# Moving an activation load off the weight queue, and sharing the last weight casts between ScalarE and VectorE, in a fused RWKV and ternary feed-forward kernel

## The chip, the cores and the metric

The kernel runs on all 8 cores of one Trainium2 chip. Each core works on its own 1024 tokens (plus 128 tokens of run-in for the recurrence), and no data passes between cores. The time is the device time of the slowest core in microseconds. Names used below: TensorE (PE in the profile), VectorE (DVE), ScalarE (ACT), GpSimd (POOL), and SyncE (SP), which only issues transfers.

## The reference

```python
xn = _layernorm(x)                                    # x: 2 x 4096 x 2048
prev = concatenate([xn[:, 1:2, :], xn[:, :-1, :]], axis=1)
xx = prev - xn
xk, xv, xr, xg = (xn + xx * tm for tm in (tm_k, tm_v, tm_r, tm_g))
r = xr @ Wr.T
k = xk @ Wk.T
v = xv @ Wv.T
g = sigmoid(xg @ Wg.T)
wkv = _wkv_scan(k, v, w, time_first)                  # recurrence over tokens
o = (sigmoid(r) * wkv * g) @ Wo.T
s = layernorm(o) * ln_g + ln_b
w_t = clip(round(weight / mean(abs(weight))), -1, 1)  # ternary weight
x = x + s * silu(xn @ (w_t * scale).T + bias)
```

All weights are 2048 x 2048 in float32, and the kernel multiplies in bfloat16.

## The kernel before

The program is a series of blocks. The first blocks compute the layernorm statistics, the mean of |weight|, and the four mixed inputs, which VectorE writes out through GpSimd's queue to the scratch tensors `sxk`, `sxv`, `sxr`, `sxg` in DRAM. Then come the two large matmul blocks that the change touches.

**The first matmul block** is `mm_group` (called at line 714). It runs three products in a row: k (weight `wk`, input `mov_kv` loaded from `sxk`), v (weight `wv`, the same buffer `mov_kv` loaded from `sxv`), and the ternary product (weight `wf`, input `xn_sb`, which is in SBUF already). Each product is done in two halves of 1024 output channels, so there are six halves. A half needs 16 weight tiles of 128 x 1024 (512 KB each). A tile is loaded into one of two staging buffers, `g1mwstg` (tile number `jj`, buffer `jj % 2`), and cast to bfloat16 into `g1wbf` (one buffer per half, two in all). In the k and v halves, even tiles are cast by VectorE (line 273) and odd ones by ScalarE (line 275). VectorE makes the ternary tiles alone (lines 265 to 270). The casts of a half may start when TensorE has finished the half before the last one (the table `release`).

One half is cut into groups: one 128-channel block by one chunk of tokens. A k or v half has 8 channel blocks of three chunks (512, 512 and 128 tokens), so 24 groups. A group is 16 matmuls into one PSUM bank, there are 8 banks, and ScalarE empties each (line 337) in order. ScalarE's program is written in order of groups: at the group at which a half's buffer comes free it first does its 8 casts of the next half's weights, then goes on emptying banks. TensorE can therefore be at most 8 groups ahead while ScalarE is at its casts.

The 16 tiles of `mov_kv` (288 KB each) are loaded in two parts. The dictionary `mov_sync={0: 8, 1: 8}` gives the first 8 tiles of each product to SyncE, counted by the semaphore `sl2`. ScalarE issues the other 8 (line 319), counted by `sl`, when it reaches the product's first group. Where SyncE's 8 stand differs: for k they are the first thing in its queue (line 213), ahead of the weight tiles; for v they come after all 32 weight tiles of v (line 220):

```python
for p, s in enumerate(specs):
    if p >= 1 and GRP0[p - 1] > 0 and movsync.get(p - 1):
        e.wait_ge(sem["smm"], b["smm"] + GRP0[p - 1])
        for ci in range(movsync[p - 1]):
            inc(e.dma_start(...), "sl2", 16)
    for h in range(2):
        ...   # the 32 weight tiles of product p, each waiting for the cast of tile jj - 2
```

TensorE waits for both counts before a product's first matmul.

**The second matmul block** (block at line 732) runs r, g and o with the weights `wr`, `wg` and `wo`. Here a slab is 512 output channels, so a product has four slabs and the block has 12. A slab is 16 weight tiles of 128 x 512 (256 KB each), in the two staging buffers `rgo_mw`, and 8 groups of 512 tokens, as many as there are PSUM banks. All 192 tiles are cast by ScalarE (line 828). ScalarE's order here is: 16 casts of the slab after next's buffer, then the 8 evictions of the slab before (lines 947, 954, 957). SyncE issues the weight tiles in order, tile `jj` after the cast of tile `jj - 2`. VectorE works through the list `v_events`: the recurrence first (`chain`, `q`, `sr`), then 32 products of `wkv` with the gate (`gmul`, line 913). The o product waits for the last of them.

After it come a layernorm of o and the final sum.

Of the kernel before, what the change touches and what calls it, by code (L numbers as in the profile page):

```python
# [23 lines left out]
def build_nc(C, T_OWN, LANE):  # L24
# [15 lines left out]
           for k in ("wk", "wv", "wr", "wg", "wo", "wf")}  # L40
# [15 lines left out]
    e0 = es0.enter_context  # L56

    sem = {n: e0(nc.semaphore(n)) for n in
           ("sl", "sl2", "sw0", "sw1", "scv", "scs", "smm", "sev", "st0",
            "st1", "sv", "ss", "sden", "srd", "sg0", "sg1")}  # L60
    cnt = {n: 0 for n in sem}

    def snap():
# [41 lines left out]
    def mm_group(specs, shared, pre=None, tail_sync=None, tail_scalar=None):  # L105
# [46 lines left out]
            CV[hh], CS[hh] = cv, cs_  # L152

        movpre = pre.get("mov_sl", {}) if pre else {}
        movsync = pre.get("mov_sync", {}) if pre else {}
        slt = {}
        slt2 = {}
        run_sl = cnt["sl"]
        run_sl2 = cnt["sl2"]
        for p, s in enumerate(specs):  # L160
            if p in movpre:
                slt[p] = movpre[p]
            elif s["mov_load"] is not None:
                run_sl += 16 * (CH - movsync.get(p, 0))
                slt[p] = run_sl
                if movsync.get(p):
                    run_sl2 += 16 * movsync[p]
                    slt2[p] = run_sl2

        signum = {}  # L170
        k = 0
# [32 lines left out]
        for p, s in enumerate(specs):  # L204
            if s["mov_load"] is not None and p not in movpre:
                mov_at.setdefault(GRP0[p], []).append(p)

        @blk.sync
        def _(e):
            for p, n in movsync.items():  # L210
                if GRP0[p] == 0:
                    for ci in range(n):
                        inc(e.dma_start(specs[p]["mov"][:, ci, :],
                                        specs[p]["mov_load"][ci, :, :]),
                            "sl2", 16)
            for p, s in enumerate(specs):
                if p >= 1 and GRP0[p - 1] > 0 and movsync.get(p - 1):
                    e.wait_ge(sem["smm"], b["smm"] + GRP0[p - 1])
                    for ci in range(movsync[p - 1]):
                        inc(e.dma_start(specs[p - 1]["mov"][:, ci, :],  # L220
                                        specs[p - 1]["mov_load"][ci, :, :]),
                            "sl2", 16)
                for h in range(2):
                    hh = 2 * p + h
                    for ic in range(CH):
                        jj = hh * CH + ic
                        if jj < preL:
                            continue
                        if jj >= 2:
                            eng, sname, tgt = castrec[jj - 2]  # L230
                            e.wait_ge(sem[sname], tgt)
                        inc(e.dma_start(mwstg[jj % 2][:, :],
                                        s["wt"][ic * 128:(ic + 1) * 128,
                                                (h * HC):(h + 1) * HC]),
                            "sw%d" % (jj % 2), 16)
            lp = len(specs) - 1
            if GRP0[lp] > 0 and movsync.get(lp):
                e.wait_ge(sem["smm"], b["smm"] + GRP0[lp])
                for ci in range(movsync[lp]):
                    inc(e.dma_start(specs[lp]["mov"][:, ci, :],  # L240
                                    specs[lp]["mov_load"][ci, :, :]),
                        "sl2", 16)
            if tail_sync is not None:
                tail_sync(e)

# [144 lines left out]
        @blk.tensor  # L390
        def _(e):
            for p, s in enumerate(specs):
                if s["mov_load"] is not None:
                    e.wait_ge(sem["sl"], slt[p])
                    if p in slt2:
                        e.wait_ge(sem["sl2"], slt2[p])
                if s.get("wait_y"):
                    e.wait_ge(sem["sv"], b["sv"] + nsig)
                for h in range(2):
                    hh = 2 * p + h  # L400
                    e.wait_ge(sem["scv"], CV[hh])
                    if CS[hh] > b0scs:
                        e.wait_ge(sem["scs"], CS[hh])
                    for oc in range(OH):
                        for tj, (t0, t1) in enumerate(s["tcs"]):
                            g = GRP0[p] + h * ngh[p] + oc * ntc[p] + tj
                            bank = ps[g % NBK]
                            if g >= NBK:
                                e.wait_ge(sem["sev"], b["sev"] + g - NBK + 1)
                            for ic in range(CH):  # L410
                                mm = e.matmul(bank[:, :t1 - t0],  # L411
                                              wbf[hh % 2][:, ic,
                                                          oc * 128:(oc + 1) * 128],
                                              s["mov"][:, ic, t0:t1],
                                              start=(ic == 0),
                                              stop=(ic == CH - 1))
                            inc(mm, "smm")
# [282 lines left out]
    with contextlib.ExitStack() as es:  # L700
        ec = es.enter_context
        mov_kv = ec(nc.sbuf_tensor("mov_kv", [128, CH, T_ALL], BF16))
        sh = {"es": es,
              "wbf": [g1wbf0,
                      ec(nc.sbuf_tensor("g1wbf1", [128, CH, HC], BF16))],
              "mwstg": g1mwstg,
              "mwm2": [ec(nc.sbuf_tensor("g1mwm2%d" % i, [128, HC], F32))
                       for i in range(2)],
              "rowst": [ec(nc.sbuf_tensor("g1row%d" % i, [128, T_ALL], F16))
                        for i in range(2)],  # L710
              "sigst": None,
              "g2st": [ec(nc.sbuf_tensor("g1g2s%d" % i, [128, 512], BF16))
                       for i in range(2)],
              "ps": [ec(nc.psum_tensor("g1ps%d" % i, [128, 512], F32))
                     for i in range(8)]}
        mm_group([
            spec(w_d["wk"], TC_ALL, "exp_row", mov_kv, mov_load=sxk,
                 store_ap=sek),
            spec(w_d["wv"], TC_ALL, "copy_row", mov_kv, mov_load=sxv,
                 store_ap=svd),  # L720
            spec(w_d["wf"], TC_OWN, "silu_g2", xn_sb, quant=True,
                 bias_vec=vec_sb["bfv"], store_ap=sg2),
        ], sh, pre=dict(preL=CH, recs=g1_pre_recs,
                        mov_sync={0: CH // 2, 1: CH // 2}))
    es_pre.close()
    es1.close()

# [4 lines left out]
    with contextlib.ExitStack() as es:  # L732
# [44 lines left out]
        CVs, CSs = [0] * NSS, [0] * NSS  # L777
        for ss in range(NSS):
            for ic in range(CH):
                cs_ += 1  # L780
                castrec.append(("S", "scs", cs_))
            CVs[ss], CSs[ss] = cv, cs_

        QLAG = 2
# [1 line left out]
        for i in range(CH + QLAG):  # L786
# [3 lines left out]
            if 0 <= cj < CH:  # L790
                v_events.append(("q", cj))
                v_events.append(("sr", cj))
        for k in range(NGp):
            v_events.append(("gmul", k))

        svord = {}
        i = 0
        for kind, l in v_events:
            if kind != "chain":
                i += 1  # L800
                svord[(kind, l)] = i
        NSV = i
# [60 lines left out]
        def _(e):  # L863
# [3 lines left out]
            for kind, l in v_events:  # L867
# [25 lines left out]
                elif kind == "q":  # L893
                    m = l % NROW
                    e.wait_ge(sem["srd"], b["srd"] + l + 1)
                    e.drain()
                    inc(e.tensor_tensor(wkv_sb[:, l, :],  # L897
                                        vvr[m][:, LANE:],
                                        ekr[m][:, LANE:],
                                        OP.mult), "sv")  # L900
                elif kind == "sr":
                    e.wait_ge(sem["sev"], b["sev"] + (l + 1) * ntc)
                    e.drain()
                    inc(e.tensor_tensor(wkv_sb[:, l, :],
                                        wkv_sb[:, l, :],
                                        sr_sb[:, l, :], OP.mult), "sv")
                else:
                    _p, sl_g, oc_g, tj_g = g_info(NR + l)
                    t0k, t1k = TC_OWN[tj_g]
                    ocg_k = sl_g * OSL + oc_g  # L910
                    e.wait_ge(sem["sev"], b["sev"] + NR + l + 1)
                    e.drain()
                    inc(e.tensor_tensor(wkv_sb[:, ocg_k, t0k:t1k],  # L913
                                        wkv_sb[:, ocg_k, t0k:t1k],
                                        sgst[l % NSG][:, :t1k - t0k],
                                        OP.mult), "sv")

        @blk.scalar
        def _(e):
# [298 lines left out]
```

## Time and profile before

| | us |
|---|---|
| median of the 2 timed runs shown | 1498.3 (1493.12 and 1503.47) |
| the profiled execution's own time | 1476.69 |
| its span, first to last instruction, slowest core (core 4) | 1475.2 |
| spans of the 8 cores | 1460.1 to 1475.2 |
| TensorE busy | 817.4 (55%) |
| VectorE busy | 524.6 (36%) |
| ScalarE busy | 494.7 (34%) |

No engine is busy for more than 55% of the span, so the table only says that engines wait for one another. Where they wait is read from the timeline. All rows are of core 4, the slowest. "SPq" and "ACTq" are the transfer instructions that SyncE and ScalarE issue; their time is that of the issuing, not of the transfer. A row's number in brackets is the idle time of the engine ahead of it and what ended it.

### The profile page before, as it was taken

To read this page: it belongs to the slowest core of one execution; us is meant where nothing else is said; L and a number is where in the kernel's file an instruction comes from. 1 tells how busy PE (TensorE), PEld (TensorE's weight loads), DVE (VectorE), ACT (ScalarE), POOL (GpSimd) and SP (SyncE) were. 2 spreads that over 40 slices of the span, in tenths; PEclk is the share of its full clock that TensorE was granted. 3 is DMA by queue.
4 is the path that set the end of the run, shared out by engine and by line. 5 is a ranking of instruction groups with operands and counts; after the bars stand their busy time and mean duration, and the time that the engine had idled before them with its cause. 6 is when DMAs were issued, how large, how long until landed. Compare 5 with 4: busy or idle time off the path is not lost. (4 is left out here: it accounts for less than half of the span.)

```text
span 1475.2 us, 11738 instructions; the slowest of 8 cores (1460.1 to 1475.2 us)
## 1 busy us (share of the span) xinstructions
PE 817.4 (55%) x3762; PEld 361.0 (24%) x3834; DVE 524.6 (36%) x499; ACT 494.7 (34%) x660; POOL 104.6 (7%) x196
## 2 busy tenths in 40 slices
PE   3532210064949049999990494561396879885200
PEld 1110000032524025554440231230142334331000
DVE  0158988200000000567304143875610000000597
ACT  5532222112122111112221355475453433328221
POOL 0002222000000000001111000000000000000011
PEclk9755555577979569999995697875698999999555
DMA  4448888664251741455216443434534444400387
GB/s 130 128 148 249 285 227 251 171 223 143 98 179 41 233 138 41 133 169 189 95 36 220 139 121 105 131 100 126 187 86 125 122 129 120 126 22 0 98 253 219
DMA packets 79070, 211.65 MB, mean 143 GB/s; under 512 B 11424, under 2 KB 11424, under 8 KB 79008
## 3 DMA queue, kind: packets, MB, share of 16 engines
q1 hardware_dynamic: 56736, 144.29, 34.0%
q0 software_dynamic: 15360, 53.49, 10.1%
q10 hardware_dynamic: 6912, 13.11, 2.6%
q8 instruction: 31, 0.51, 0.1%
q14 instruction: 31, 0.25, 0.1%
HBM read 166.81 MB, written 39.85 MB: 140 GB/s over the span
## 5 line engine op out<-in xcount | busy, mean ns | idle before, releaser
L981 PE MATMUL rgo_ps<-mov_rg,rgo_wbf 128*128 128x512 bf16 x1003 | 235.7, 396 | 184.2 <-ACT rgo_wbf L828 57.6
L411 PE MATMUL g1ps<-mov_kv,g1wbf 128*128 128x512 bf16 (+1 forms) x1505 | 255.1, 330 | 138.1 <-DMA mov_kv<-sxv 57.0
L828 ACT ACTIVATE rgo_wbf<-rgo_mw 128x512 bf16<-128x512 f32 x192 | 119.9, 633 | 266.5 <-DMA rgo_mw<-wr 92.0
L411 PEld LDWEIGHTS g1ps<-mov_kv,g1wbf 128*128 128x128 bf16 x1536 | 131.5, 100 | 261.7 <-issue 144.4
L981 PEld LDWEIGHTS rgo_ps<-mov_rg,rgo_wbf 128*128 128x128 bf16 x1024 | 103.4, 102 | 316.4 <-issue 206.1
L981 PE MATMUL rgo_ps<-wkv_sb,rgo_wbf 128*128 128x512 bf16 x502 | 116.2, 392 | 19.7 <-ACT sr_sb L957 11.2
L411 PE MATMUL g1ps<-xn_sb,g1wbf 128*128 128x512 bf16 x502 | 110.1, 379 | 0.5
L337 ACT ACTIVATE g1row<-g1ps 128x512 f16<-128x512 f32 (+1 forms) x96 | 45.3, 492 | 173.9 <-PE g1ps L411 165.2
L273 DVE CAST g1wbf<-g1mwstg 128x1024 bf16<-128x1024 f32 x24 | 16.7, 694 | 241.1 <-PE g1ps L411 91.9
L579 PE MATMUL ps_sc<-fs_a,ones 128*1 128x512 f16 x64 | 32.3, 608 | 83.1 <-ACT fs_a L624 83.1
L981 PEld LDWEIGHTS rgo_ps<-wkv_sb,rgo_wbf 128*128 128x128 bf16 x512 | 51.1, 100 | 84.7 <-issue 28.7
L411 PEld LDWEIGHTS g1ps<-xn_sb,g1wbf 128*128 128x128 bf16 x512 | 50.1, 98 | 60.2
L275 ACT ACTIVATE g1wbf<-g1mwstg 128x1024 bf16<-128x1024 f32 x24 | 25.3, 1056 | 108.6 <-DMA g1mwstg<-wv 72.0
L265 DVE TENSOR_SCALAR g1mwm<-g1mwstg,thr_sb 128x1024 f32<-128x1024 f32 x32 | 24.1, 754 | 104.2 <-PE g1ps L411 83.6
L624 ACT ACTIVATE fs_a<-g1mwstg 128x1024 f16<-128x1024 f32 x32 | 33.7, 1057 | 80.1 <-DMA g1mwstg<-wf 80.1
L897 DVE TENSOR_TENSOR wkv_sb<-r_vvr,r_ekr 128x1024 bf16<-128x1024 f16 x16 | 11.1, 692 | 137.3 <-ACT r_ekr L940 136.4
L1046 DVE TENSOR_SCALAR stm<-qs 1x512 f32<-1x512 f32 x2 | 1.3, 674 | 162.7 <-PE qs L1037 162.7
L344 ACT ACTIVATE g1g2s<-g1ps,v_bfv,scale_sb 128x512 bf16<-128x512 f32 x32 | 24.9, 778 | 81.7 <-PE g1ps L411 81.7
L913 DVE TENSOR_TENSOR wkv_sb<-wkv_sb,rgo_sg 128x512 bf16<-128x512 bf16 x32 | 13.6, 425 | 91.3 <-ACT rgo_sg L954 88.4
L521 PE MATMUL ps<-xh,ones 128*1 128x512 f16 (+1 forms) x48 | 23.9, 497 | 34.3 <-ACT xq L508 34.3
L879 DVE TENSOR_TENSOR_SCAN zar<-w_sb,r_vvr 128x1152 f32<-128x1152 f32 x16 | 40.9, 2559 | 1.5 <-issue 0.4
L881 DVE TENSOR_TENSOR_SCAN zbr<-w_sb,r_ekr 128x1152 f32<-128x1152 f32 x16 | 40.5, 2533 | 0.0
(112 smaller groups left out, 841.7 us busy)
## 6 DMA issues: line engine op xcount, KB each, us to landing
g1mwstg<-wf SPq DMA_DIRECT2D x64, 512.0 KB, 4.7
g1mwstg<-wk SPq DMA_DIRECT2D x32, 512.0 KB, 5.6
g1mwstg<-wv SPq DMA_DIRECT2D x32, 512.0 KB, 4.8
rgo_mw<-wr SPq DMA_DIRECT2D x64, 256.0 KB, 3.4
rgo_mw<-wg SPq DMA_DIRECT2D x64, 256.0 KB, 3.2
rgo_mw<-wo SPq DMA_DIRECT2D x64, 256.0 KB, 3.2
xstg<-x SPq DMA_DIRECT2D x16, 576.5 KB, 3.9
xst<-x SPq DMA_DIRECT2D x16, 512.0 KB, 5.1
```

The lines of the kernel that those rows point to most:

```text
L265: e.tensor_single_scalar(mwm2[jj % 2][:, :], mwstg[jj % 2][:, :], thr_sb[:, :], OP.is_gt)
L275: e.activation(dstsl, mwstg[jj % 2][:, :], AF.Copy).then_inc(sem["scs"], 1)
L337: inc(e.activation(rowst[ro % 2][:, t0:t1], bank[:, :t1 - t0], fn), "sev")
L344: inc(e.activation(g2st[gk % 2][:, :t1 - t0], bank[:, :t1 - t0], AF.Silu, bias=s["bias_vec"][:, ocg:ocg + 1], scale=scale_sb[:, 0:1]), "sev")
L411: mm = e.matmul(bank[:, :t1 - t0], wbf[hh % 2][:, ic, oc * 128:(oc + 1) * 128], s["mov"][:, ic, t0:t1], start=(ic == 0), stop=(ic == CH - 1))
L521: e.matmul(ps1[j][:, :t1 - t0], ones16[:, :], xh16[:, ci, t0:t1], start=(ci == 0), stop=(ci == CH - 1))
L579: mm = e.matmul(ps_sc[:, :q1 - q0], ones16[:, :], habs[sl_ % 2][:, q0:q1], start=(sl_ == 0 and j == 0), stop=(sl_ == NSL - 1 and j == len( ...
L624: inc(e.activation(habs[sl_ % 2][:, :], g1mwstg[sl_ % 2][:, :], AF.Abs), "scv")
L828: e.activation(wbf[ss % 2][:, ic, :], mwstg[jj % 2][:, :], AF.Copy).then_inc(sem["scs"], 1)
L879: e.tensor_tensor_scan(zar[:, 1:], wbc, vvr[m][:, :], 0.0, OP.mult, OP.add)
L881: e.tensor_tensor_scan(zbr[:, 1:], wbc, ekr[m][:, :], 0.0, OP.mult, OP.add)
L981: mm = e.matmul(bank[:, :t1 - t0], wbf[ss % 2][:, ic, oc * 128:(oc + 1) * 128], phs[p]["mov"][:, ic, t0:t1], start=(ic == 0), stop=(ic == ...
```

## The change

It has two parts. In the first matmul block the call loses `mov_sync`, so all 16 tiles of `mov_kv` are issued by ScalarE at a product's first group, and the semaphore `sl2` goes. In the second block the casts of the four `wo` slabs (the last product) are shared: VectorE casts the even tiles and ScalarE the odd ones. VectorE's casts are sorted in among the gate products by the group at which they may start; at a tie the gate product goes first.

```diff
-        movsync = pre.get("mov_sync", {}) if pre else {}
...
-                run_sl += 16 * (CH - movsync.get(p, 0))
+                run_sl += 16 * CH
                 slt[p] = run_sl
-                if movsync.get(p):
-                    run_sl2 += 16 * movsync[p]
-                    slt2[p] = run_sl2
...
                     e.wait_ge(sem["sl"], slt[p])
-                    if p in slt2:
-                        e.wait_ge(sem["sl2"], slt2[p])
...
-        ], sh, pre=dict(preL=CH, recs=g1_pre_recs,
-                        mov_sync={0: CH // 2, 1: CH // 2}))
+        ], sh, pre=dict(preL=CH, recs=g1_pre_recs))
...
             for ic in range(CH):
-                cs_ += 1
-                castrec.append(("S", "scs", cs_))
+                if ss >= 2 * NSLAB and ic % 2 == 0:
+                    cv += 1
+                    castrec.append(("V", "scv", cv))
+                else:
+                    cs_ += 1
+                    castrec.append(("S", "scs", cs_))
...
-        for k in range(NGp):
-            v_events.append(("gmul", k))
+        tail_ev = [(NR + k + 1, 0, ("gmul", k)) for k in range(NGp)]
+        for jj in range(NSS * CH):
+            if castrec[jj][0] == "V":
+                tail_ev.append((release[jj // CH], 1, ("vcast", jj)))
+        tail_ev.sort(key=lambda t: (t[0], t[1]))
+        v_events += [ev for _, _, ev in tail_ev]
...
+                else:
+                    emit_cast(e, l)
```

SyncE's queue through the first matmul block, before. `mov_kv` is the input buffer, `g1mwstg` the weight staging:

```order
L213 DMA mov_kv<-sxk 128x1152 x8
L232 DMA g1mwstg<-wk 128x1024 x16
L232 DMA g1mwstg<-wv 128x1024 x32
L220 DMA mov_kv<-sxv 128x1152 x8
L232 DMA g1mwstg<-wf 128x1024 x32
```

And now:

```order
L228 DMA g1mwstg<-wk 128x1024 x16
L228 DMA g1mwstg<-wv 128x1024 x32
L228 DMA g1mwstg<-wf 128x1024 x32
```

Both pieces of 8 are gone from SyncE: the one ahead of k's weights and the one behind v's. ScalarE's order at the beginning of v was:

```order
L337 ACTIVATE g1row<-g1ps 128x128
L319 DMA mov_kv<-sxv 128x1152 x8
L275 ACTIVATE g1wbf<-g1mwstg 128x1024 x8
L337 ACTIVATE g1row<-g1ps 128x512 x2
L337 ACTIVATE g1row<-g1ps 128x128
```

And now:

```order
L333 ACTIVATE g1row<-g1ps 128x128
L315 DMA mov_kv<-sxv 128x1152 x16
L271 ACTIVATE g1wbf<-g1mwstg 128x1024 x8
L333 ACTIVATE g1row<-g1ps 128x512 x2
L333 ACTIVATE g1row<-g1ps 128x128
```

The eight transfers stand in ScalarE's queue, ahead of its eight casts. VectorE's order from the last of the recurrence to the end of the second block, before:

```order
L904 TENSOR_TENSOR wkv_sb<-wkv_sb,sr_sb 128x1024
L897 TENSOR_TENSOR wkv_sb<-r_vvr,r_ekr 128x1024
L904 TENSOR_TENSOR wkv_sb<-wkv_sb,sr_sb 128x1024
L913 TENSOR_TENSOR wkv_sb<-wkv_sb,rgo_sg 128x512 x32
L732 UNCONDITIONAL_BRANCH
```

And now:

```order
L905 TENSOR_TENSOR wkv_sb<-wkv_sb,sr_sb 128x1024
L898 TENSOR_TENSOR wkv_sb<-r_vvr,r_ekr 128x1024
L905 TENSOR_TENSOR wkv_sb<-wkv_sb,sr_sb 128x1024
L914 TENSOR_TENSOR wkv_sb<-wkv_sb,rgo_sg 128x512 x24
L826 CAST rgo_wbf<-rgo_mw 128x512 x8
L914 TENSOR_TENSOR wkv_sb<-wkv_sb,rgo_sg 128x512 x8
L826 CAST rgo_wbf<-rgo_mw 128x512 x24
L725 UNCONDITIONAL_BRANCH
```

Eight casts (the first `wo` slab) stand ahead of the last eight gate products, the other 24 behind them. On ScalarE the four pieces of 16 casts for `wo` become pieces of 8 at the same places.

## Rows read from the trace of the kernel before

**Rows 1.** Waits: engine and line waited for, total us, times, longest us.

```profile
PE g1ps L411 <- DMA mov_kv<-sxv: 57.0, 1, 57.0
...
PE g1ps L411 <- ACT g1row L337: 41.8, 2, 21.8
```

**Rows 2.** Timeline, beginning of v: start us, us, engine line, what.

```profile
478.22 4.58 ACTq L319 DMA_DIRECT2D mov_kv<-sxv  x8
...
482.96 1.06 ACT L275 ACTIVATE g1wbf<-g1mwstg 128x1024 bf16<-128x1024 f32 x1 [4.47 <-issue]
...
490.99 1.06 ACT L275 ACTIVATE g1wbf<-g1mwstg 128x1024 bf16<-128x1024 f32 x1 [6.97 <-DMA g1mwstg<-wv]
...
521.26 5.87 SPq L220 DMA_DIRECT2D mov_kv<-sxv  x8
...
535.13 45.16 PE L411 MATMUL g1ps<-mov_kv,g1wbf 128*128 128x512 bf16 x255 [57.02 <-DMA mov_kv<-sxv]
...
599.54 0.75 DVE L265 TENSOR_SCALAR g1mwm<-g1mwstg,thr_sb 128x1024 f32<-128x1024 f32 x1 [74.81 <-PE g1ps L411]
```

**Rows 3.** Timeline, first half of k.

```profile
285.56 6.20 ACTq L319 DMA_DIRECT2D mov_kv<-sxk  x8
...
306.25 24.24 PE L411 MATMUL g1ps<-mov_kv,g1wbf 128*128 128x512 bf16 x125 [37.72 <-DMA mov_kv<-sxk]
...
308.01 1.28 ACT L275 ACT_TABLE_LOAD   x1 [27.86 <-DMA g1mwstg<-wk]
...
309.31 1.06 ACT L275 ACTIVATE g1wbf<-g1mwstg 128x1024 bf16<-128x1024 f32 x1
...
348.81 1.06 ACT L275 ACTIVATE g1wbf<-g1mwstg 128x1024 bf16<-128x1024 f32 x1 [4.30 <-DMA g1mwstg<-wk]
...
392.53 0.69 DVE L273 CAST g1wbf<-g1mwstg 128x1024 bf16<-128x1024 f32 x1 [45.81 <-PE g1ps L411]
```

**Rows 4.** Windows: stretch, us, busy us of PE, PEld, DVE, ACT, POOL, then PEclk, DMA share, GB/s.

```profile
350.00:392.50 42.50, 41.74 (x253) 22.25 (x259) 0.00 (x0) 10.43 (x24) 3.78 (x7) 0.95 0.18 66
478.00:499.00 21.00, 0.11 (x2) 0.00 (x0) 2.08 (x3) 3.45 (x4) 0.54 (x1) 0.56 0.80 259
```

**Rows 5.** Timeline, beginning of the second block: ScalarE issues 16 input tiles.

```profile
781.30 12.52 ACTq L927 DMA_DIRECT2D mov_rg<-sxr  x16
```

**Rows 6.** DMA issues from 285.5 to 306 us: count, KB each, median us to landing.

```profile
g1mwstg<-wk SPq DMA_DIRECT2D x2, 512.0 KB, 15.4
```

**Rows 7.** Part 6 of the page, weight tiles: the same columns, whole run.

```profile
g1mwstg<-wv SPq DMA_DIRECT2D x32, 512.0 KB, 4.8
...
rgo_mw<-wo SPq DMA_DIRECT2D x64, 256.0 KB, 3.2
```

**Rows 8.** Timeline, the `wo` slabs.

```profile
1194.76 4.00 ACT L954 ACTIVATE rgo_sg<-rgo_ps 128x512 bf16<-128x512 f32 x8
...
1195.50 4.05 DVE L913 TENSOR_TENSOR wkv_sb<-wkv_sb,rgo_sg 128x512 bf16<-128x512 bf16 x8 [28.81 <-ACT rgo_sg L954]
...
1199.91 29.87 PE L981 MATMUL rgo_ps<-wkv_sb,rgo_wbf 128*128 128x512 bf16 x126 [7.80 <-ACT rgo_wbf L828]
...
1229.76 4.00 ACT L957 ACTIVATE sr_sb<-rgo_ps 128x512 bf16<-128x512 f32 x8
...
1233.58 1.21 ACT L828 ACTIVATE rgo_wbf<-rgo_mw 128x512 bf16<-128x512 f32 x2
...
1263.76 0.63 ACT L828 ACTIVATE rgo_wbf<-rgo_mw 128x512 bf16<-128x512 f32 x1 [1.39 <-DMA rgo_mw<-wo]
1264.29 4.00 ACT L957 ACTIVATE sr_sb<-rgo_ps 128x512 bf16<-128x512 f32 x8
...
1297.78 4.00 ACT L957 ACTIVATE sr_sb<-rgo_ps 128x512 bf16<-128x512 f32 x8
```

**Rows 9.** Groups of instructions by line, shapes apart: count, busy us, mean ns, idle before.

```profile
L273 DVE CAST g1wbf<-g1mwstg 128x1024 bf16<-128x1024 f32 x24 | 16.7, 694 | 241.1 <-PE g1ps L411 91.9 <-DMA g1mwstg<-wv 75.0 <-DMA g1mwstg<-wk 74.2
...
L913 DVE TENSOR_TENSOR wkv_sb<-wkv_sb,rgo_sg 128x512 bf16<-128x512 bf16 x32 | 13.6, 425 | 91.3 <-ACT rgo_sg L954 88.4 <-issue 0.4
```

More of the change, by code:

```diff
@@ L58, in build_nc @@
     sem = {n: e0(nc.semaphore(n)) for n in
-           ("sl", "sl2", "sw0", "sw1", "scv", "scs", "smm", "sev", "st0",
-            "st1", "sv", "ss", "sden", "srd", "sg0", "sg1")}
+           ("sl", "sw0", "sw1", "scv", "scs", "smm", "sev", "st0", "st1",
+            "sv", "ss", "sden", "srd", "sg0", "sg1")}
     cnt = {n: 0 for n in sem}
@@ L154, in mm_group @@
         movpre = pre.get("mov_sl", {}) if pre else {}
-        movsync = pre.get("mov_sync", {}) if pre else {}
         slt = {}
-        slt2 = {}
         run_sl = cnt["sl"]
-        run_sl2 = cnt["sl2"]
         for p, s in enumerate(specs):
@@ L206, in mm_group @@
                 mov_at.setdefault(GRP0[p], []).append(p)
+        movsync = pre.get("mov_sync", {}) if pre else {}
         @blk.sync
@@ L214, in _ @@
                                         specs[p]["mov_load"][ci, :, :]),
-                            "sl2", 16)
+                            "sl", 16)
             for p, s in enumerate(specs):
@@ L221, in _ @@
                                         specs[p - 1]["mov_load"][ci, :, :]),
-                            "sl2", 16)
+                            "sl", 16)
                 for h in range(2):
@@ L241, in _ @@
                                     specs[lp]["mov_load"][ci, :, :]),
-                        "sl2", 16)
+                        "sl", 16)
             if tail_sync is not None:
@@ L798, in build_nc @@
         for kind, l in v_events:
-            if kind != "chain":
+            if kind not in ("chain", "vcast"):
                 i += 1
@@ L906, in _ @@
                                         sr_sb[:, l, :], OP.mult), "sv")
-                else:
+                elif kind == "gmul":
                     _p, sl_g, oc_g, tj_g = g_info(NR + l)
```

## The prediction

> **What bounds the kernel now.** I read the table of busy times first: TensorE works in 817.4 of 1475.2 us, so the end is set by what it waits for. The second view is the list of waits for the first matmul block [rows 1]. TensorE waits once for 57.0 us for v's input, and twice for some 21 us (41.8 in all) for ScalarE to empty a bank. The third is the timeline at those places.
>
> At the beginning of v [rows 2] ScalarE issues its 8 input tiles at 478.22 and then begins its casts of v's second half. SyncE comes to its own 8 only at 521.26, when nearly all of those 16 weight tiles have gone through. TensorE starts at 535.13. So the 57 us are not the time of a transfer; they are the place in SyncE's queue. VectorE's first ternary cast, which waits for the end of v's first half, stands at 599.54: this is where a gain in v shows.
>
> At the beginning of k [rows 3] TensorE starts at 306.25 and works 24.24 us, which is 8 groups, then stands until ScalarE has done its last cast (348.81, and 1.06 us long). After that cast the first eviction frees a bank. From there, at 349.87, the other 16 groups need until 392.53, which is 42.7 us. I call the end of ScalarE's casts E: a half of k or v ends at E + 42.7, as long as TensorE has 8 groups done by E. The granted clock in that stretch is 0.95 [rows 4], so the return from the half clock is inside the 42.7.
>
> **Part one: v.** Removed: SyncE's wait and 8 issues. Added: 8 issues on ScalarE, ahead of its casts. Eight cost 4.58 us there [rows 2]; 16 cost 9.2 by that row. The row of another place has 12.52 us for 16 [rows 5]. The first cast moves from 482.96 to 478.22 + 9.2 + 0.2 = 487.6 (at the worst 490.9). SyncE can load an odd weight tile only after ScalarE's cast of the one before, so what follows is seven cycles of load and cast. A cycle with input tiles in flight took 490.99 - 482.96 = 8.0 us [rows 2], one without (348.81 - 309.31) / 7 = 5.64 us [rows 3]. How many are long: 16 tiles of 288 KB are 4.7 MB, with about 1 MB of weights 5.7 MB; at the 259 GB/s of 478 to 499 us [rows 4] that is 22 us, so the input is in at about 500.
>
> - Best: one long cycle, E = 487.6 + 8.0 + 6 x 5.64 + 1.06 = 530.5.
> - Worst by these rows: issue 12.5 us and three long cycles, E = 490.9 + 24.1 + 4 x 5.64 + 1.06 = 538.6.
> - I take 534.5, by 9.2 us of issue and two long cycles (532.9) with 1.6 us towards the worse end, since twice as many input tiles share the first cycles.
>
> TensorE starts at 500 and has its 8 groups at 500.3 + 24.2 = 524.5, 10 us ahead of E. So the half ends at 534.5 + 42.7 = 577.2 in place of 599.54: **22.3 us** less (18.2 to 26.3). What hides the later input load is exactly this: ScalarE is at its casts until E anyway. What follows (v's second half, the ternary halves, whose casts are VectorE's) has no wait that a shift could fall into: nothing there depends on absolute time.
>
> **Part one: k.** Here the 8 tiles were at the head of SyncE's queue, so the input itself comes no earlier; what comes earlier is the weights behind it. Two weight tiles that were issued behind the input took 15.4 us to land [rows 6] against 4.8 usually [rows 7]. Now they are issued first. ScalarE is busy with issues for 2 x 6.20 = 12.4 us [rows 3], so its first cast comes at 285.56 + 12.4 + 1.28 (table load) = 299.3 in place of 309.31. One long cycle and six short ones: E = 299.3 + 8.0 + 6 x 5.64 + 1.06 = 342.2 against 349.87, 7.7 us. The other end: if the second pair of weight tiles needs 15.4 us too, that cycle is 15.4 + 1.2 = 16.6 and the first cast comes at 301, so E = 352.5 and 2.6 us are lost. At best all of 309.31 - 299.3 = 10.0 is kept. I take **7.0 us**, near the row of v's cycle, which was measured with the input and the weights in flight together. TensorE may start up to 6.2 us later (312.5) and still has 8 groups at 336.7, before E.
>
> The Trainium skill speaks against expecting anything here ("DMA: Bandwidth & Descriptors", section "Issuing engines are not separate DMA queues"): transfers from several engines run on the same 16 DMA engines, and spreading the issue saves only the issue time. By that rule alone, giving up SyncE as second issuer costs 6.2 us in k and 4.6 in v and gains nothing, if the input load sets the end. The rows agree about the sharing; the gain I count comes from the place in the queue, and the input load of both products ends while ScalarE is still casting.
>
> **Part two: the `wo` casts.** In this block ScalarE does 16 casts, then 8 evictions in 4.00 us, and TensorE can't go more than 8 groups ahead. The period is ScalarE's: 1194.76, 1229.76, 1264.29, 1297.78 [rows 8], so 35.0, 34.5 and 33.5 us, where TensorE needs 29.87 for a slab. The time is not cast time: the 16 casts are 16 x 0.63 = 10 us of some 30. ScalarE waits for the next tile. Its odd tiles come every (1263.76 - 1234.2) / 7 = 4.2 us, of which 3.2 is the landing [rows 7] and 0.63 the cast. With the even tiles on VectorE the odd ones still go load, cast, load, and SyncE still issues in order. What goes is the wait of the odd tile behind the even cast, and VectorE can work ahead by one tile while ScalarE empties banks. I take a cycle of 4.0 us: period 4.00 + 0.63 + 7 x 4.0 = 32.6, which gains 2.4 + 1.9 + 0.9 = 5.2. Against it: in the slab cast from 1198.8 on, VectorE is at its gate products until 1195.50 + 4.05 = 1199.55, 0.8 us after ScalarE would have cast. That leaves 4.4, and I take **4.5 us**. The first `wo` slab gains nothing for the same reason. VectorE's cast of 512 columns isn't in the trace: it lies between half of the 694 ns for 1024 columns and 694, near the 425 ns of another operation on 512 columns [rows 9]; any of these is under ScalarE's 630 and on no path. Bounds: with cycles that stay at 4.2 the sum is about -2 (the delays behind the gate products); if the casts no longer bind and TensorE's 29.87 does, 5.1 + 4.6 + 3.6 = 13.3.
>
> **Sum.** 22.3 + 7.0 + 4.5 = 33.8 us. Against the profiled execution's 1476.69 us that is 1442.9. That execution was 21.6 us under the median of the two timed runs, 1498.3; nothing in the change touches this difference, so I forecast 1498.3 - 33.8 = **1464.5 us**.
>
> **The rivals.**
>
> 1. The input load starves the weights in both products. For it: the 15.4 us landing [rows 6]. Against: the cycle of 8.0 us in v, with 8 input tiles in flight. Two cycles of 16.6 in v give E = 490.9 + 33.2 + 5 x 5.64 + 1.06 = 553.4, so a gain of 3.4; k loses 2.6; with 4.5 of part two 5.3 in all: 1493.
> 2. Only the place in the queue counts, at the worst prices above: v 18.2, k 4, `wo` nothing: 22 us, 1476. For it: cycles in `wo` are load latency, which sharing a cast doesn't shorten. This is also the case in which part two does not do what it says.
> 3. `wo` becomes bound by TensorE: 22.3 + 7.0 + 13.3 = 42.6, 1456. For it: ScalarE is freed of half its casts. Against: it was waiting, not casting.
> 4. Slower: handing tiles to two engines in turn has its own period. The only rows of alternating casts are k's and v's, 5.64 us a cycle [rows 3]. Should `wo` take that, each of the 4 slabs loses 7 x (5.64 - 4.2) = 10 us, 40 in all, against 29.3 gained in part one: 1498.3 + 11 = 1509. It decides from a cycle of 4.2 + 29.3 / 28 = 5.2 us on. Against it: those tiles have twice the bytes and land in 4.8 us rather than 3.2 [rows 7]; that 1.6 us alone accounts for the 1.44 us between the two cycles.
>
> **How the numbers follow.** The forecast gets 0.60, rival 1 0.10, rival 2 0.17, rival 3 0.09, rival 4 0.04. The forecast's own range is a gain of 26 to 42 us. 2% of 1498.3 is 30 us, about what a measurement of this kernel can tell from no change, and the gain stands just over it. Faster by over 2%: 0.8 of the forecast's 0.60 (0.48), rival 3 (0.09), and a little of rival 2, so 0.59. Slower by over 2% needs rival 4 with a worse price still: 0.03. The rest is 0.38. The range holds the forecast, rivals 2 and 3, and half of the 21.6 us between the two kinds of run shown, on either side: 1440 to 1488.
>
> **What would show it.** In the profile after: TensorE waits for v's input for some 22 us, not 57, and then a third wait of about 10 us for ScalarE's evictions appears; ScalarE's last cast before v ends 56 us after v's input is first issued; in k the last cast ends 57 us after the issue of the input, not 64. ScalarE's four blocks of evictions in `wo` stand 32 to 33 us apart. VectorE has 32 casts more. The forecast is wrong if v's input comes after 524, if the cycles of load and cast beside the input exceed 10 us, or if the period in `wo` doesn't fall.

## The result, and the profile after

| | before | after |
|---|---|---|
| median of all timed runs, us | 1489.02 (10 runs, 1478.2 to 1503.47) | 1459.28 (11 runs, 1452.98 to 1492.66) |
| profiled execution, us | 1476.69 | 1452.98 |
| its span, slowest core | 1475.2 (core 4) | 1451.4 (core 6) |

After to before is 0.9805, with the interval 0.9767 to 0.9844: 29 us less, between 23 and 35. Some executions of every kernel here are longer because one die of four cores, at times both, runs at a lower clock (after's 1492.66 is one); the ratios leave them out, and e2_k_only, with three of four of this kind, its profile among them, has none. The forecast was 1464.5 from a base of 1498.3, 33.8 us less. The forecast's gain lay just over 2% and the measured one just under it; the interval has that line inside, so on which side the gain lies is not settled.

The waits for the first matmul block in the profile after, in the columns of [rows 1]:

```profile
PE g1ps L405 <- DMA mov_kv<-sxk: 43.8, 1, 43.8
PE g1ps L405 <- ACT g1row L333: 38.4, 3, 24.8
PE g1ps L405 <- DMA mov_kv<-sxv: 24.5, 1, 24.5
```

The 57.0 us of [rows 1] are 24.5, and the waits for ScalarE's evictions are three, not two. The wait for k's input grew from 37.7 [rows 3] to 43.8. The timeline of core 6 after, beginning of v (before: [rows 2]; the row at 533.78 ends with its window, at 600 us):

```profile
478.43 11.06 ACTq L315 DMA_DIRECT2D mov_kv<-sxv  x16
489.65 1.06 ACT L271 ACTIVATE g1wbf<-g1mwstg 128x1024 bf16<-128x1024 f32 x1 [10.96 <-issue]
498.94 1.06 ACT L271 ACTIVATE g1wbf<-g1mwstg 128x1024 bf16<-128x1024 f32 x1 [8.24 <-DMA g1mwstg<-wv]
504.55 1.06 ACT L271 ACTIVATE g1wbf<-g1mwstg 128x1024 bf16<-128x1024 f32 x1 [4.56 <-DMA g1mwstg<-wv]
...
502.85 25.22 PE L405 MATMUL g1ps<-mov_kv,g1wbf 128*128 128x512 bf16 x128 [24.54 <-DMA mov_kv<-sxv]
...
532.10 1.06 ACT L271 ACTIVATE g1wbf<-g1mwstg 128x1024 bf16<-128x1024 f32 x1 [4.77 <-DMA g1mwstg<-wv]
533.06 2.38 ACT L333 ACTIVATE g1row<-g1ps 128x512 f16<-128x512 f32 x6
533.78 66.52 PE L405 MATMUL g1ps<-mov_kv,g1wbf 128*128 128x128 bf16 x403 [5.71 <-ACT g1row L333]
...
576.44 0.75 DVE L261 TENSOR_SCALAR g1mwm<-g1mwstg,thr_sb 128x1024 f32<-128x1024 f32 x1 [46.40 <-PE g1ps L405]
```

All 16 tiles are issued at once, TensorE starts at 502.85 and not at 535.13, does its 128 matmuls (8 groups of 16) and stands 5.7 us until ScalarE's last cast is done at 533.16. The first ternary cast comes 98.0 us after the issue of v's input; before it was 599.54 - 478.22 = 121.3. The same for k (before: [rows 3]):

```profile
284.59 15.67 ACTq L315 DMA_DIRECT2D mov_kv<-sxk  x16
...
300.34 1.28 ACT L271 ACT_TABLE_LOAD   x1 [19.25 <-issue]
301.64 1.06 ACT L271 ACTIVATE g1wbf<-g1mwstg 128x1024 bf16<-128x1024 f32 x1
...
310.60 1.06 ACT L271 ACTIVATE g1wbf<-g1mwstg 128x1024 bf16<-128x1024 f32 x1 [7.90 <-DMA g1mwstg<-wk]
...
314.74 25.41 PE L405 MATMUL g1ps<-mov_kv,g1wbf 128*128 128x512 bf16 x128 [43.81 <-DMA mov_kv<-sxk]
...
346.30 1.06 ACT L271 ACTIVATE g1wbf<-g1mwstg 128x1024 bf16<-128x1024 f32 x1 [5.37 <-DMA g1mwstg<-wk]
```

Here 16 issues take 15.67 us, and the last cast ends 62.8 us after the first issue, where before it was 64.3. And the `wo` slabs (before: [rows 8]):

```profile
1141.90 4.00 ACT L957 ACTIVATE rgo_sg<-rgo_ps 128x512 bf16<-128x512 f32 x8
...
1176.36 4.00 ACT L957 ACTIVATE rgo_sg<-rgo_ps 128x512 bf16<-128x512 f32 x8
1177.09 4.04 DVE L914 TENSOR_TENSOR wkv_sb<-wkv_sb,rgo_sg 128x512 bf16<-128x512 bf16 x8 [2.74 <-ACT rgo_sg L957]
1181.61 58.22 PE L984 MATMUL rgo_ps<-wkv_sb,rgo_wbf 128*128 128x512 bf16 x256 [9.51 <-DVE rgo_wbf L826]
1210.13 4.00 ACT L960 ACTIVATE sr_sb<-rgo_ps 128x512 bf16<-128x512 f32 x8
1243.67 4.00 ACT L960 ACTIVATE sr_sb<-rgo_ps 128x512 bf16<-128x512 f32 x8
1244.40 29.92 PE L984 MATMUL rgo_ps<-wkv_sb,rgo_wbf 128*128 128x512 bf16 x128 [4.57 <-ACT sr_sb L960]
1276.04 4.00 ACT L960 ACTIVATE sr_sb<-rgo_ps 128x512 bf16<-128x512 f32 x8
```

The periods are 33.8, 33.5 and 32.4, 99.7 together, where [rows 8] have 35.0, 34.5 and 33.5, 103.0. The means of the 8 cores are 34.0, 32.5 and 32.5 after and 34.2, 34.8 and 34.0 before. What both casting engines wait for there, in the view of waits after:

```profile
DVE rgo_wbf L826 <- DMA rgo_mw<-wo: 102.5, 29, 4.2
...
ACT rgo_wbf L829 <- DMA rgo_mw<-wo: 94.8, 27, 5.0
```

Each is idle for some 100 us for weight tiles. VectorE's 32 casts cost it only 13.7 us:

```profile
L826 DVE CAST rgo_wbf<-rgo_mw 128x512 bf16<-128x512 f32 x32 | 13.7, 427 | 106.0 <-DMA rgo_mw<-wo 102.5 <-PE rgo_ps L984 3.6
```

One core is a weak basis for terms of a few us, since a period differs by a us or two between cores. So I read the same distances from the timelines of all 8 cores of each profile and took means. "k" is from the issue of k's input to ScalarE's first eviction, "k all" to the issue of v's input, "v" from there to the first ternary cast, "to r" from there to the issue of r's input, "r" from there to the issue of g's, "g" from there to the first `wo` matmul, "o" from there to the layernorm of o. All in us:

```
                  k    k all      v     to r      r       g       o
before          64.5   192.8   120.3   183.7   258.9   160.6   130.6
after           59.8   188.7    96.9   183.1   258.5   162.0   125.7
e1_v_only       63.9   193.4    98.0   185.2   260.4   160.7   130.1
e2_k_only       58.9   187.9   121.0   185.6   260.5   162.8   131.4
e3_wo_only      63.3   192.7   120.9   186.1   259.6   164.2   126.6
e4_v_early_sync 64.2   193.7   101.0   182.9   258.9   161.0   129.7
e5_wo_all_v     59.4   189.1    97.6   184.9   261.7   159.7   122.9
e6_kv_all_v     35.5   155.6    93.6   182.0   258.8   161.8   129.0
e8_four_buffers 59.2   188.0    98.8   183.4   201.5   132.6   112.9
e9_kv_v_four    35.8   155.9    93.0   181.9   201.8   131.8   112.9
```

After against before: k all 4.1, v 23.4, o 4.9, and g loses 1.4. With 0.6 and 0.4 in the two others the sum is 32.0. Columns that an edit doesn't touch differ by up to 3 us between profiles; smaller differences in one column say nothing. The 1.4 us of g are such a difference.

TensorE's own waits in k and v, as means of the 8 cores: the wait for v's input fell from 55.6 to 23.9 us; the wait for an eviction in k's first half from 21.0 to 8.1; the one in the middle of k is 21.2 before and 21.6 after; v's new wait for an eviction is 6.1.

### The profile page after: what moved, and what is told of

Read it like the earlier page. It is cut to its first block and busy times, and to the rows that moved or that the text cites. A ratio compares the mean times of both kernels' runs of the same rounds, so it can differ in the third digit from the quotient of the medians.

```text
span 1451.4 us, 11811 instructions; the slowest of 8 cores (1427.7 to 1451.4 us)
## 1 busy us (share of the span) xinstructions
PE 823.4 (57%) x3834; PEld 361.9 (25%) x3834; DVE 538.1 (37%) x531; ACT 474.3 (33%) x628; POOL 104.7 (7%) x196
## 3 DMA queue, kind: packets, MB, share of 16 engines
q0 software_dynamic: 15360, 53.49, 10.3%
## 5 line engine op out<-in xcount | busy, mean ns | idle before, releaser
L405 PE MATMUL g1ps<-mov_kv,g1wbf 128*128 128x512 bf16 (+1 forms) x1536 | 261.0, 335 | 106.7 <-DMA mov_kv<-sxk 43.8
L829 ACT ACTIVATE rgo_wbf<-rgo_mw 128x512 bf16<-128x512 f32 x160 | 100.2, 632 | 284.3 <-DMA rgo_mw<-wo 94.8
L984 PEld LDWEIGHTS rgo_ps<-wkv_sb,rgo_wbf 128*128 128x128 bf16 x512 | 51.1, 100 | 81.4 <-issue 24.5
L826 DVE CAST rgo_wbf<-rgo_mw 128x512 bf16<-128x512 f32 x32 | 13.7, 427 | 106.0 <-DMA rgo_mw<-wo 102.5
L266 DVE TENSOR_TENSOR g1wbf<-g1mwm,g1mwstg 128x1024 bf16<-128x1024 f32 x32 | 39.2, 1225 | 2.7 <-issue 0.4
```

The costliest lines, as they stand in the source:

```text
L266: e.tensor_tensor(dstsl, mwm2[jj % 2][:, :], mwstg[jj % 2][:, :], OP.subtract).then_inc(sem["scv"], 1)
L405: mm = e.matmul(bank[:, :t1 - t0], wbf[hh % 2][:, ic, oc * 128:(oc + 1) * 128], s["mov"][:, ic, t0:t1], start=(ic == 0), stop=(ic == CH - 1))
L829: e.activation(wbf[ss % 2][:, ic, :], mwstg[jj % 2][:, :], AF.Copy).then_inc(sem["scs"], 1)
L984: mm = e.matmul(bank[:, :t1 - t0], wbf[ss % 2][:, ic, oc * 128:(oc + 1) * 128], phs[p]["mov"][:, ic, t0:t1], start=(ic == 0), stop=(ic == ...
```

## The experiments

Each was timed beside the kernel before (median 1495.99 of 13 runs beside the first four, 1498.32 of 7 runs beside the others). The ratios are to it.

**e1_v_only.** The kernel before, with all of v's input on ScalarE and the rest left.

```diff
-                        mov_sync={0: CH // 2, 1: CH // 2}))
+                        mov_sync={0: CH // 2}))
```

> Undoes all of the change but v's part: SyncE keeps its 8 input tiles of k, v's 16 are all issued by ScalarE, wo casts stay on ScalarE. Theory (v's input stood behind the weights in SyncE's queue, and this carries most of the gain): 22 to 24 us under the kernel before; from the issue of v's input to the first ternary cast 97 us instead of 121; k's stage (input issue to first eviction) unchanged at about 64. Rival (v's gain is given back later, the whole gain is k and wo): within 5 us of the kernel before.

Measured 1472.22 us, ratio 0.9823 (0.9751 to 0.9896), and v at 98.0 in place of 120.3. So 22.3 us of the change lie in v, by this edit alone. k stayed at 63.9.

**e2_k_only.** The same for k alone.

```diff
-                        mov_sync={0: CH // 2, 1: CH // 2}))
+                        mov_sync={1: CH // 2}))
```

> Only k's part: k's 16 input tiles on ScalarE, v's 8 stay behind the weights on SyncE. Theory (weights go first, ScalarE's casts end earlier): k's input issue to first eviction falls from 64.5 to about 60 us (mean of the cores), total 4 to 7 us faster. Rival (the 16 issues on ScalarE hold its casts as long as the earlier weights gain, the differences seen are spread between cores): 0, within 2 us.

Measured 1493.34 us (1470.57 to 1497.4, four runs), with no ratio: the total decides nothing. By the stages, k is at 58.9 and "k all" at 187.9 in place of 192.8: 4.9 us, not 7. The timeline of its core 2, where both the issue and the cycle beside the input are the longest of the 8 cores:

```profile
283.40 15.60 ACTq L319 DMA_DIRECT2D mov_kv<-sxk  x16
...
300.37 1.06 ACT L275 ACTIVATE g1wbf<-g1mwstg 128x1024 bf16<-128x1024 f32 x1
311.72 1.06 ACT L275 ACTIVATE g1wbf<-g1mwstg 128x1024 bf16<-128x1024 f32 x1 [10.29 <-DMA g1mwstg<-wk]
317.22 1.06 ACT L275 ACTIVATE g1wbf<-g1mwstg 128x1024 bf16<-128x1024 f32 x1 [4.45 <-DMA g1mwstg<-wk]
```

16 issues take 15.60 us, and the cycle beside the input takes 11.35; the next is 5.5. The means of the 8 cores are 12.7 and 9.2.

**e3_wo_only.** The kernel before, with the new sharing of the `wo` casts alone (second and third part of the diff).

```diff
+                if ss >= 2 * NSLAB and ic % 2 == 0:
+                    cv += 1
+                    castrec.append(("V", "scv", cv))
...
```

> Only the wo casts shared. Theory (the period is the latency of loading a tile, the cast is a small part): the three periods between ScalarE's blocks of evictions sum to about 99 instead of 103 us, total 4 to 5 us faster. Rival (ScalarE's casts are the bound): periods at TensorE's 30 us, 13 us faster. Second rival: no gain.

Measured 1490.97 us, ratio 0.9972 (0.9933 to 1.0011): about 4 us, and nothing isn't excluded. The stage o fell from 130.6 to 126.6, the three periods in it from 103.0 to 100.1 together (means of the 8 cores). g stood 3.6 higher, but 2.9 of these come before its second block of evictions and so ahead of any `wo` cast: they are not the edit's.

**e4_v_early_sync.** The kernel before, with SyncE still the issuer of 8 tiles of v, but two weight tiles into v's second half and no longer behind all its weights. This holds the place in the queue apart from the engine that issues.

```diff
-                if p >= 1 and GRP0[p - 1] > 0 and movsync.get(p - 1):
-                    e.wait_ge(sem["smm"], b["smm"] + GRP0[p - 1])
...
+                        if (h == 1 and ic == 2 and GRP0[p] > 0
+                                and movsync.get(p)):
+                            e.wait_ge(sem["smm"], b["smm"] + GRP0[p])
...
```

> The kernel before with one thing moved: SyncE still issues 8 of v's input tiles, but after the second weight tile of v's second half instead of after the sixteenth. Theory (the place in the queue, not the issuing engine): the same gain as with all on ScalarE, 20 to 26 us; ScalarE issues only 8 and starts its casts 4.6 us earlier, SyncE's next weight tiles wait some 5 us behind its 8 issues. Rival (SyncE's issues are what delays, wherever they stand): under 12 us.

Measured 1464.86 us, ratio 0.9805 (0.9741 to 0.9869), v at 101.0. The timeline of its core 4:

```profile
475.07 6.54 SPq L227 DMA_DIRECT2D mov_kv<-sxv  x8
475.11 6.81 ACTq L320 DMA_DIRECT2D mov_kv<-sxv  x8
...
481.71 50.21 SPq L233 DMA_DIRECT2D g1mwstg<-wv  x14
482.08 1.06 ACT L276 ACTIVATE g1wbf<-g1mwstg 128x1024 bf16<-128x1024 f32 x1 [6.71 <-issue]
...
497.88 24.42 PE L412 MATMUL g1ps<-mov_kv,g1wbf 128*128 128x512 bf16 x128 [22.88 <-DMA mov_kv<-sxv]
...
500.66 1.06 ACT L276 ACTIVATE g1wbf<-g1mwstg 128x1024 bf16<-128x1024 f32 x1 [17.52 <-DMA g1mwstg<-wv]
```

The 57 us are 22.9 with SyncE still issuing: it was the place in the queue. As a mean of the 8 cores TensorE waits 20.6 us for v's input here, 24.2 in e1 and 23.9 after, so a second issuer brings it 3 to 4 us earlier; the issues take 5.3 us in place of 9.9. That is the Trainium skill's rule ("DMA: Bandwidth & Descriptors", section "Issuing engines are not separate DMA queues"), by which a second issuing engine saves only the time of initiating: the trace agrees, with 3.6 us of the 4.6 that the issues are shorter. The rule is silent about the 34 us that the same eight transfers cost by standing behind weights that wait for casts.

Yet v ends 3 us later here than in e1 (101.0 and 98.0). SyncE's next weight tiles, issued from 481.71 on behind the input, come so late that ScalarE's next cast waits until 500.66: one cycle of 18.6 us, 17.7 as a mean of the cores, where e1 has a longest one of 9.7 and the expectation had some 5 us of delay. VectorE's next cast stands at 499.39, 24.2 us after the one before; in the kernel after (core 6) it is 9.3 us. So rival 1's mechanism exists: weights that are issued behind the input are starved.

**e5_wo_all_v.** The kernel after, with all `wo` tiles cast by VectorE. If the sharing is worth what ScalarE's casts cost, going on should give nothing or a loss; if only latency and order count, VectorE alone is as good.

```diff
-                if ss >= 2 * NSLAB and ic % 2 == 0:
+                if ss >= 2 * NSLAB:
```

> The changed kernel with all wo tiles cast by VectorE, so that ScalarE has no casts ahead of its evictions there. Theory (a period is eight cycles of load and cast, whichever engine casts): the casts of a slab still take about 30 us; only ScalarE's 4 us of evictions drop out of the period, so the three periods fall from 99 to about 91 us, but the first slab's casts now hold up the last 8 gate products, and the total is 2 to 6 us under the changed kernel. Rival (ScalarE's casts were the bound): periods at TensorE's 28 to 29.5, 13 us under it.

Measured 1455.49 us, ratio 0.9702 (0.9593 to 0.9811) against before; the interval overlaps that of the kernel after. The stage o is at 122.9, 2.8 less than after, and g at 159.7. ScalarE no longer empties banks in blocks there, so the periods of the expectation can't be read off. VectorE has 32 casts more than after, ScalarE 32 fewer, and nothing is lost: the cast time of neither engine binds there.

**e6_kv_all_v.** The kernel after, with all casts of k and v on VectorE, so that ScalarE only empties banks.

```diff
-                        if specs[p]["quant"] or ic % 2 == 0:
+                        if True:
```

> The changed kernel with all k and v tiles cast by VectorE. Theory (TensorE's waits of 8 to 22 us in k and v are ScalarE's casts standing ahead of its evictions in program order, limited to 8 banks): these waits vanish, each half takes 62 to 64 us, the waits that stay are those for the input. About 43 us under the changed kernel, 73 under the kernel before. Rival (the weight tiles' arrival holds TensorE, not the order on ScalarE): no gain over the changed kernel.

Measured 1423.81 us, ratio 0.9505 (0.9431 to 0.9579). TensorE's whole timeline through k and v, core 1:

```profile
322.19 126.36 PE L405 MATMUL g1ps<-mov_kv,g1wbf 128*128 128x512 bf16 x768 [46.94 <-DMA mov_kv<-sxk]
480.09 120.24 PE L405 MATMUL g1ps<-mov_kv,g1wbf 128*128 128x512 bf16 x722 [31.54 <-DMA mov_kv<-sxv]
```

Once the input is in, k and v run through without a stop (the second row ends with its window, at 600 us). "k all" fell by 33.1 and v by 3.3 against after, 36 together; 43 were expected. This tests the prediction's E: with no casts ahead of the evictions nothing waits for E. The rival, that faster casts did it, is out: v's first half takes 43.9 us from the first cast to the end of the last here and 43.3 after, and k's last cast ends 56.9 us after the issue of k's input in place of 59.9 (means of the 8 cores). TensorE's three waits for evictions after, 8.1, 21.6 and 6.1 us, add up to the 36 gained. v had only the last of them to give, and its input came 5 us later here (a wait of 28.9 us, not 23.9). k has more, because two blocks of casts stand in it. The second, the casts for v's first half, comes in the middle of k, in the timeline of the kernel after:

```profile
390.02 1.06 ACT L271 ACTIVATE g1wbf<-g1mwstg 128x1024 bf16<-128x1024 f32 x1
...
435.16 1.06 ACT L271 ACTIVATE g1wbf<-g1mwstg 128x1024 bf16<-128x1024 f32 x1 [5.33 <-DMA g1mwstg<-wv]
...
436.85 41.46 PE L405 MATMUL g1ps<-mov_kv,g1wbf 128*128 128x128 bf16 x256 [24.84 <-ACT g1row L333]
```

No bank is emptied for 46 us, and TensorE stands 24.8 of them. That wait was there before too (21.8 in [rows 1]); the change doesn't touch it.

**e8_four_buffers.** The kernel after, with four staging buffers in the second matmul block, each with its own semaphore.

```diff
...
-                if jj >= 2:
-                    eng, sname, tgt = castrec[jj - 2]
+                if jj >= 4:
+                    eng, sname, tgt = castrec[jj - 4]
...
```

> The changed kernel with four staging buffers instead of two in the second block (four weight tiles in flight). Theory (the periods in the second block are tile latency: with twice the tiles in flight the casts of a slab take about 16 to 20 us instead of 30): the wo periods fall to TensorE's 28 to 30 us, the first wait of the block (60 us) falls by 15 or more, total 40 to 80 us under the changed kernel. Rival (bandwidth bound: the DMA engines are shared and full): under 10 us.

Measured 1370.08 us (1346.77 to 1408.22), ratio 0.9029 (0.8866 to 0.9192). Against after r has 57.0 less, g 29.4 and o 12.8: 99 us, more than the 40 to 80 expected. The block's first wait, for the first slab's casts, gave less than expected: it fell from 58.9 to 49.6 us (means of the 8 cores). The timeline of core 6, and one window of its o product:

```profile
1100.36 110.67 PE L986 MATMUL rgo_ps<-wkv_sb,rgo_wbf 128*128 128x512 bf16 x502 [1.79 <-ACT rgo_wbf L831]
```

```profile
1100.00:1180.00 80.00, 79.27 (x362) 36.15 (x370) 9.78 (x24) 25.15 (x45) 0.00 (x0) 1.00 0.49 145
```

The four slabs are one run of 110.67 us, 27.7 each, at full clock (the granted clock is 1.00 in that window). Now TensorE is the bound there, which two buffers never let it be: the same kind of window of the kernel after is

```profile
1185.00:1265.00 80.00, 75.43 (x335) 33.40 (x334) 8.97 (x21) 20.16 (x36) 0.00 (x0) 0.94 0.44 129
```

**e9_kv_v_four.** e6 and e8 in one kernel.

> Both of the above together (k and v casts on VectorE, four staging buffers in the second block). The two act in different blocks, so if both theories hold the gains add up: 80 to 120 us under the changed kernel. If the cores of a pair meet in memory bandwidth, less than the sum.

Measured 1314.59 us (1306.11 to 1330.47), ratio 0.874 (0.8601 to 0.8878). Each stage is within 0.8 us of the one of e6 or e8 that it comes from, so the two edits add up. The median is 145 us under after's, more than the 80 to 120 expected.

## Why the prediction came out as it did

- **v, 22.3 forecast, 23.4 measured (22.3 in e1).** The step "they are the place in SyncE's queue" is shown by e1 and e4. Its parts came out as follows in core 6: input in at 502.85 (forecast 500); the third wait of TensorE 5.7 us (forecast 10); the last cast 533.16 - 478.43 = 54.7 us after the issue (forecast 56). Two errors met: the issue took 11.06 us and not 9.2, but there was one long cycle (9.3 us), where I took two of 8.0 and 1.6 us on top. The half ended 43.3 us after E, against the 42.7 used. One of the signs of being wrong did come: the long cycle is over 10 us in 4 of the 8 cores (10.3 to 11.0), and in k in 2. In v it cost nothing, since only one cycle is long (9.6 and six others of 5.5 as means of the cores).
- **k, 7.0 forecast, 4.1 measured (4.9 in e2).** The mechanism held: k's weights go first now. The size was off, in E = 299.3 + 8.0 + 6 x 5.64 + 1.06. By the means of the 8 cores the last cast ends 59.9 us after the first issue and not 56.6: the issues took 13.3 us and not 12.4, the long cycle 9.3 and not 8.0, the six short ones 34.8 and not 33.8. So each term is some 1 us short, and none of them makes the miss alone. In core 6 the issues are the largest part: 15.67 us, 3.3 more than forecast, of 6.2 in all. The prediction had the 12.52 us row at hand [rows 5], which showed that an issue can cost 0.78 us, and used it only as v's worst case.
- **`wo`, 4.5 forecast, 4.9 measured in o (3.5 with the 1.4 of g, which is within the scatter).** The cycle of ScalarE's odd tiles fell as said in two of the three periods: from 4.27 to 4.00 us and from 4.16 to 4.02 (means of the 8 cores), and with it the periods to 32.5, against 32.6 forecast. In the first period it stayed (4.20, then 4.23), so that period is 34.0, where the forecast with its 0.8 us behind the gate products has 33.4. Why it stayed wasn't tried. Nothing is lost at the gate products: from ScalarE's last block of their evictions to TensorE's start of `wo` it is 5.1 us before and 5.2 after. By itself (e3) the part is worth 4.0 in o, while the total's interval runs from 2 us lost to 10 gained. The prediction's lower bound, "the sum is about -2", doesn't follow from its terms: periods of 4.00 + 0.63 + 7 x 4.2 = 34.0 give 1.0 + 0.5 - 0.5, and 0.2 after the 0.8.
- **What the sum was made from.** 33.8 forecast, 29.7 between the medians, 32.0 by stages. The parts are 1.1 too low, 2.9 too high and 0.4 too low, so the sum is nearer than k alone. The base of 1498.3 was a median of two runs; with ten it is 1489.02, 9.3 lower. The forecast time is only 5.2 us off because this and a gain 4.1 too large partly cancel: that is luck. The range's lower end is 1445 by its own terms (rival 3's 1456 less 10.8), not 1440. I carried the 21.6 us between the profiled execution and the median of two through to the forecast. After, the profiled execution is 6 us under its median; the difference was mostly the spread of runs and belongs to no stage.
- **The rivals.** Rival 1 fell: one cycle in v is long, not two of 16.6; its mechanism shows only in e4, in one cycle. Rival 2 had k right (4) and v and `wo` too low. Rival 3 fell: TensorE bounds `wo` only with four buffers (e8). Rival 4 fell: the hand-off between engines gave no period of 5.64; e5, without any hand-off, is not slower and scarcely faster. That ScalarE's 5.64 us in k is the latency of the larger tile was an argument; e8, where only the number of tiles in flight was changed, shows that latency is what binds in the second block.

Open: why the same 16 issues cost 9.9 us in v and 13.3 in k (means of the 8 cores) was not tried. Four staging buffers in the first block were not tried either.

## What to carry to other kernels

A long wait for a small transfer is first to be looked up in its issuer's queue: what stands ahead of it there, and what does that wait for? When both casting engines are idle for the same tiles, sharing the casts bought a few us here, and another pair of buffers brought the stage down to TensorE's own time. And casts that stand ahead of PSUM evictions in one engine's order hold TensorE as soon as it has filled its banks; here they belonged on the engine that empties none (e6).

## What the runs showed of the hardware

The cost of issuing one transfer from ScalarE varied with the place: 0.57 us for v's tiles before [rows 2], 0.69 after (11.06 / 16), 0.78 for k's before [rows 3] and for r's [rows 5], 0.98 for k's after.

It varied as much between cores. Over the 8 cores after, k's 16 issues took 10.0 to 16.0 us and v's 8.8 to 11.5. In each pair of neighbouring cores (0 and 1, 2 and 3, and so on) the core that comes to them later, counted from its own first instruction, took longer: for k 16.0, 14.6, 15.0 and 15.7 us, beside 13.1, 10.4, 10.0 and 11.8. Over the ten profiles and the inputs of k, v and r this holds in 116 of 120 pairs. Before, k's 8 issues took 6.0 to 6.2 us in one core of each pair and 3.9 to 4.4 in the other; the prediction's 6.20 is one of the first kind. What the two cores share isn't shown.

The two rows of 16 beside busy DMA engines are these windows of the kernel after (columns as in [rows 4]):

```profile
284.50:306.00 21.50, 0.00 (x0) 0.00 (x0) 1.39 (x2) 2.34 (x2) 0.00 (x0) 0.50 0.90 235
```

```profile
478.00:500.00 22.00, 0.31 (x6) 0.14 (x3) 1.39 (x2) 2.50 (x4) 0.54 (x1) 0.56 0.91 278
```

The DMA engines are equally busy in both (0.90 and 0.91), so their share alone doesn't say why k's cost more. And twice as many weight tiles in flight made one land only a little later. The DMA issues of the `wo` stage, after and then in e8:

```profile
rgo_mw<-wo SPq DMA_DIRECT2D x41, 256.0 KB, 3.3
```

```profile
rgo_mw<-wo SPq DMA_DIRECT2D x44, 256.0 KB, 3.9
```

Landing went from 3.3 to 3.9 us (median, in the two windows of e8's section). The DMA share rose only from 0.44 to 0.49, since TensorE sets the pace there with four buffers, so how much more the queue could carry isn't shown.
